# Layer 1 of a two-layer graph attention kernel: the probabilities of 3 of 12 chunks are split in row layout and turned by DMA

## Chip, cores and metric

One core of one Trainium2 chip. The metric is device time in microseconds of the whole launch, lower is better.

## The reference, cut to what matters

```python
x = _layernorm(x + L0(x, L0_gnn_input, adj, L0_gnn_weight))     # x: 6144 x 128, adj: 6144 x 6144
x = _layernorm(x + L1(x, adj, L1_gnn_W, L1_gnn_a1, L1_gnn_a2))

def L0(xx_anchor, input, adj, weight):
    anchor_adj = jnp.einsum('md,de,ne->mn', xx_anchor, weight, input)
    scores = jnp.where(adj > 0, anchor_adj, -2 ** 32 + 1)
    return jax.nn.softmax(scores / 0.07, axis=1) @ input
```

The change lies in L0, which is called layer 1 here (the first of two). Each of its 6144 rows has a softmax over 6144 masked scores and a product of these probabilities with `input`.

## The kernel before

**Layer 1** goes over 48 row tiles of 128 rows. A tile has 6144 scores per row, cut into 12 chunks of 512 (`C = 12`, `CHUNK = 512`, `BPC = 4` blocks of 128 per chunk). Every engine runs its own program (`tile_steps`, on GpSimd `tile_rstd`, on SP `load_tile`) with a body for each tile t and steps c = 0 to 11 in it; semaphores alone couple them, and an engine that waits holds up all that stands behind. One body holds work of three tiles.

- TensorE, `tile_steps` (L484): in step c it turns one chunk of probabilities of an earlier tile (4 transposes through the identity, L502, two PSUM banks `NPT`), makes the scores of chunk c of tile t (L513 to L515, three float16 products, four banks), then the value products of an earlier chunk (`attend`, L467: four times L478 and L480). A chunk of tile t-1 is turned three steps after it would be its turn (`LAG`, `turn_of` L252), and its products follow two steps later (`PV_LAG`). The turn waits for `pT_lo_set` of the chunk two before, which frees its bank. In step 5 it turns the next tile's x (L443).
- ScalarE (L642): copies the turned chunk to float16 (`pT_hi`, L659), then the exponential of chunk c of tile t-1, in place in `rows` (L665, with a sum). In step 5 it copies the finished product out of PSUM (`att`, L653).
- VectorE (L786): on odd c it adds the mask to a pair of score chunks, writes them to `rows` and keeps their maximum (L801). Then `pT_lo` = turned chunk minus `pT_hi` (L810). Then, spread over the steps, masks from the adjacency (L778, steps 0, 2, 4, 10), the sum of probabilities and its inverse (L828, L830, step 3), that inverse over 64 (L833, step 5), residual sums into `xr` (L839, L843, steps 6 and 7), statistics (L847 to L852, step 8), `x1` (L855, step 9), row maximum and exponential's bias (L860, L864, step 11).
- GpSimd, `tile_rstd` (L379): turns each quarter of the mask into bytes (`make_edges`, L360), the power -0.5 for the layer norm (L388), and products for layer 2's scores with a running total (`score_cols`, L371, L377).
- SP: loads x and adj, stores the edge bytes, all in one queue and in the order written (`load_tile`, L294).

**Layer 2** (from about 1070 us) reads the edge bytes back with 48 transposing DMAs (`edgesT`, L322), VectorE makes weights (L891), ScalarE and GpSimd split them (L694, L404), TensorE multiplies. The change doesn't touch it.

Of the kernel before, what the change touches and what calls it, by code (L numbers as in the profile page):

```python
# [10 lines left out]
PT_SLOTS = 4  # L11
PV_LAG = 2
PARTS = 8
PART_SLOTS = 4
# [21 lines left out]
def build(nc, x, adj, inp, w0, w1, a1, a2, edge_rows, out):  # L36
# [17 lines left out]
    with ExitStack() as ctx:  # L54
# [5 lines left out]
        def sem(name):  # L60
            return ctx.enter_context(nc.semaphore(name))
# [28 lines left out]
        pT_hi = sb0("pT_hi", [P, PT_SLOTS, CHUNK], F16)  # L90
        pT_lo = sb0("pT_lo", [P, PT_SLOTS, CHUNK], F16)
        xq = sb0("xq", [P, P], F32)
        xr = sb0("xr", [P, 2, P], F32)
# [115 lines left out]

        x_turned, xT_hi_set, xT_lo_set = sem("x_turned"), sem("xT_hi_set"), sem("xT_lo_set")  # L210
        att_out = sem("att_out")
        max_set, bias_set = sem("max_set"), sem("bias_set")
# [36 lines left out]
        def z_bank(c):  # L249
            return ps[:, (PV, MISC)[c % 2], :]  # L250

        def turn_of(t, c):  # L252

            return (1, c - LAG) if c >= LAG else (2, C - LAG + c)

        def tiles(eng, body):

            for t in range(NB + 2):
                body(t, t % 2, t)
# [4 lines left out]
        def turn_at(known, c):  # L264
            if known is None:
                return True
            off, _ = turn_of(known, c)
            return 0 <= known - off < NB

        def ends_tile(known):  # L270
            return known is None or known >= 2

# [3 lines left out]
        def _(sp):  # L276
# [13 lines left out]
            def store_edges(t, q):  # L290
                sp.wait_ge(edges_set, QUARTERS * t + q + 1)
                sp.dma_start(pair_rows(edge_rows, t)[:, q * QW // 2:(q + 1) * QW // 2], edges[:, q, :]).then_inc(edges_out[q], 16)

            def load_tile(t, par, known):  # L294
                if scores_of(known) and known != 0:

                    after(sp, x_turned, t)
                    sp.dma_start(xq[:], pair_rows(x, t)).then_inc(xq_in, 16)
                    for q in range(QUARTERS):

                        after(sp, mask_set, QUARTERS * (t - 1) + q + 1)
                        sp.dma_start(adj_sb[:, q, :], pair_rows(adj, t)[:, q * QW:(q + 1) * QW]).then_inc(adj_in[q], 16)
                        store_edges(t - 1, q)
                if known == NB:
                    for q in range(QUARTERS):
                        store_edges(t - 1, q)
                if known is None or 1 <= known <= NB:

                    after(sp, x1_set, t - 2)
                    sp.dma_start(xr[:, 1 - par, :], pair_rows(x, t - 1)).then_inc(xr_in[1 - par], 16)  # L310

# [27 lines left out]
        def _(pool):  # L339
# [26 lines left out]
            def score_cols(j):  # L366
# [8 lines left out]
                else:  # L375
                    pool.wait_ge(total_set, j)
                    nc.gpsimd.tensor_tensor(x1_total[:], x1_total[:], x1, ALU.add).then_inc(total_set, 1)  # L377

            def tile_rstd(t, par, known):  # L379
                ahead = t < NB - 1  # L380
                if t < NB:
                    for q in range(QUARTERS // 2, QUARTERS):
                        make_edges(t, q)
                if ahead:
                    make_edges(t + 1, 0)
                if ends_tile(known):
                    pool.wait_ge(ve_set, t - 1)
                    nc.gpsimd.tensor_tensor(small[:, 4:5], small[:, 3:4], consts[:, 0:1], ALU.pow).then_inc(rstd_set, 1)  # L388
                    score_cols(t - 2)
                if ahead:  # L390
                    make_edges(t + 1, 1)
# [36 lines left out]
        def _(pe):  # L428
# [38 lines left out]
            def attend(t_of, bc):  # L467

                n = C * t_of + bc
                pe.wait_ge(pT_lo_set, n + 1)  # L470
                if bc == 0:
                    after(pe, att_out, t_of)
                acc = ps[:, PV, 0:2 * P]
                s = bc % PT_SLOTS
                for b in range(BPC):
                    jb = bc * BPC + b
                    cols = slice(b * P, (b + 1) * P)
                    nc.tensor.matmul(acc, pT_hi[:, s, cols], vals[:, jb, :], start=(jb == 0), stop=False,  # L478
                                     skip_group_check=True)
                    mm = nc.tensor.matmul(acc[:, P:2 * P], pT_lo[:, s, cols], vals[:, jb, 0:P], start=False,  # L480
                                          stop=(jb == NB - 1), skip_group_check=True)
                mm.then_inc(pv_done, 1)

            def tile_steps(t, par, known):  # L484
                for c in range(C):
# [8 lines left out]
                    if turn_at(known, c):  # L494

                        off, bc = turn_of(t, c)
                        pb = par if off == 2 else 1 - par
                        n = C * (t - off) + bc
                        pe.wait_ge(exp_set, C * (t - off) + bc + 1)
                        after(pe, pT_lo_set, n + 1 - NPT)  # L500
                        for b in range(BPC):
                            mm = nc.tensor.transpose(ps[:, PT0 + bc % NPT, b * P:(b + 1) * P],  # L502
                                                     rows[:, pb * N + bc * CHUNK + b * P:pb * N + bc * CHUNK + (b + 1) * P],
                                                     ident[:])
# [12 lines left out]

                    if c < PV_LAG:
                        if known is None or known >= 1 and turn_at(known - 1, C + c - PV_LAG):
                            off, bc = turn_of(t, C + c - PV_LAG)  # L520
                            attend(t - off - 1, bc)
                    elif turn_at(known, c - PV_LAG):
                        off, bc = turn_of(t, c - PV_LAG)
                        attend(t - off, bc)
                    if c == x_step(known) and (known is None or known < NB - 1):
# [86 lines left out]
        def _(act):  # L612
# [29 lines left out]
            def tile_steps(t, par, known):  # L642
                for c in range(C):
                    if known == 0:
                        if c + Z_LEAD + 1 < C:
                            inpT_out(c + Z_LEAD + 1)
                        if c + Z_LEAD < C:
                            z_high(c + Z_LEAD)
                    if c == LAG + PV_LAG and ends_tile(known):

# [3 lines left out]
                    if turn_at(known, c):  # L654
                        off, bc = turn_of(t, c)
                        n = C * (t - off) + bc
                        act.wait_ge(turned, n + 1)
                        after(act, pv_done, n + 1 - PT_SLOTS)
                        nc.scalar.copy(pT_hi[:, bc % PT_SLOTS, :], ps[:, PT0 + bc % NPT, :]).then_inc(pT_hi_set, 1)  # L659
                    if known is None or 1 <= known <= NB:  # L660
# [7 lines left out]
                    if c == x_step(known) and (known is None or known < NB - 1):  # L668
                        xT_high(t + 1, 1 - par)
                    if c == 11 and ends_tile(known):  # L670
                        score_sums(t - 2)

# [75 lines left out]
        def _(dve):  # L748
# [37 lines left out]
            def tile_steps(t, par, known):  # L786
                for c in range(C):
# [5 lines left out]
                    if scores_of(known) and c % 2 == 1:  # L793

                        k = c // 2
                        dve.wait_ge(mask_set, QUARTERS * t + c // QC + 1)
                        after(dve, turned, C * (t - 2) + c + 1 if t >= 2 else 0)
                        if k == 0:
# [5 lines left out]
                    if turn_at(known, c):  # L804

                        off, bc = turn_of(t, c)
                        n = C * (t - off) + bc
                        dve.wait_ge(pT_hi_set, n + 1)
                        s = bc % PT_SLOTS
                        nc.vector.tensor_tensor(pT_lo[:, s, :], ps[:, PT0 + bc % NPT, :], pT_hi[:, s, :],  # L810
                                                ALU.subtract).then_inc(pT_lo_set, 1)
# [13 lines left out]
                    if ends_tile(known):  # L825
# [5 lines left out]
                        if c == 5:  # L831
                            dve.wait_ge(inv_set, t - 1)
                            nc.vector.tensor_scalar(small[:, 2:3], small[:, 1:2], 1.0 / SPLIT_SCALE, None,  # L833
                                                    ALU.mult).then_inc(scaled_set, 1)
                        if c == 6:
                            dve.wait_ge(scaled_set, t - 1)
# [3 lines left out]
                                                           in1=xr[:, par, :], op0=ALU.mult, op1=ALU.add).then_inc(u1_set, 1)  # L840
                        if c == 7:
                            dve.wait_ge(u1_set, t - 1)
                            nc.vector.scalar_tensor_tensor(out=xr[:, par, :], in0=att[:, P:2 * P], scalar=small[:, 2:3],  # L843
                                                           in1=xr[:, par, :], op0=ALU.mult, op1=ALU.add).then_inc(u_set, 1)
                        if c == 8:
                            dve.wait_ge(u_set, t - 1)
                            nc.vector.bn_stats(stats[:], xr[:, par, :]).then_inc(stats_set, 1)  # L847
                            dve.wait_ge(stats_set, t - 1)
                            nc.vector.bn_aggr(moments[:], stats[:]).then_inc(moments_set, 1)
                        if c == 8:  # L850
                            dve.wait_ge(moments_set, t - 1)
                            nc.vector.tensor_scalar(small[:, 3:4], moments[:, 1:2], EPS, None, ALU.add).then_inc(ve_set, 1)  # L852
                        if c == 9:
                            dve.wait_ge(rstd_set, t - 1)
                            nc.vector.tensor_scalar(x1_all[:, t - 2, :], xr[:, par, :], moments[:, 0:1], small[:, 4:5], ALU.subtract,  # L855
                                                    ALU.mult).then_inc(x1_set, 1)
                    if c == C - 1 and scores_of(known):
# [148 lines left out]
```

## Time and profile before

| | |
|---|---|
| median of 3 runs | 1553.66 us (1552.51 to 1554.07) |
| profiled execution | 1552.38 us, its span 1550.5 us |
| TensorE, VectorE, ScalarE, GpSimd busy | 97%, 89%, 70%, 56% of the span |
| DMA | 241 MB, mean 156 GB/s |
| layer 1, layer 2 | up to about 1070 us, about 480 us |

In the profile PE is TensorE, DVE VectorE, ACT ScalarE, POOL GpSimd and SPq the DMA queue of SP. Busy time is the time in which an engine executes; a matmul's end is modelled, and since matmuls are pipelined, the distance between two starts tells more than a duration. The same holds for VectorE, where an instruction's start overlaps the end of the one before by some 0.08 us.

### The profile page before, as it was taken

To read this page: it belongs to the slowest core of one execution; us is meant where nothing else is said; L and a number is where in the kernel's file an instruction comes from. 1 tells how busy PE (TensorE), PEld (TensorE's weight loads), DVE (VectorE), ACT (ScalarE), POOL (GpSimd) and SP (SyncE) were. 2 spreads that over 40 slices of the span, in tenths; PEclk is the share of its full clock that TensorE was granted. 3 is DMA by queue.
4 is the path that set the end of the run, shared out by engine and by line. 5 is a ranking of instruction groups with operands and counts; after the bars stand their busy time and mean duration, and the time that the engine had idled before them with its cause. 6 is when DMAs were issued, how large, how long until landed. Compare 5 with 4: busy or idle time off the path is not lost.

```text
span 1550.5 us, 29603 instructions
## 1 busy us (share of the span) xinstructions
PE 1499.2 (97%) x10429; PEld 1091.5 (70%) x10429; DVE 1383.3 (89%) x2447; ACT 1078.5 (70%) x2423; POOL 864.1 (56%) x580
## 2 busy tenths in 40 slices
PE   6799999999999999999999999997999999999996
PEld 3577777777777777777777777775556666666664
DVE  7999999999999999999999999986869797979794
ACT  3577777777777777777777777777745554546463
POOL 5333344333344333344333343323999999999995
PEclk9999999999999999999999999998999999999998
DMA  7655566555566555565555565524333535353520
GB/s 244 217 166 179 204 211 210 184 173 179 205 211 207 181 175 183 206 211 204 182 173 185 207 211 200 178 74 98 82 65 79 115 62 116 72 109 82 105 61 14
DMA packets 228226, 241.13 MB, mean 156 GB/s; under 512 B 157168, under 2 KB 203504, under 8 KB 228080
## 3 DMA queue, kind: packets, MB, share of 16 engines
q1 hardware_dynamic: 228080, 239.25, 49.9%
q8 instruction: 84, 1.38, 0.4%
q14 instruction: 62, 0.51, 0.1%
HBM read 160.56 MB, written 40.89 MB: 130 GB/s over the span
## 4 chain that ended last, share of the span: by engine, by line
PE 90%; POOL 3%; issue 2%; DVE 1%; ACT 1%; ACTq 0%; POOLq 0%; DVEq 0%
PE ps L502 16%; PE ps L478 16%; PE ps L566 11%; PE ps L559 10%; PE ps L480 8%; PE ps L515 8%; PE ps L514 8%; PE ps L513 8%; PE ps L543 5%; POOL p_lo L404 2%; PE ps L577 1%; POOL vals_lo L400 1%; PE ps L443 0%; PE ps L536 0%; POOL s_prod L371 0%
## 5 line engine op out<-in xcount | busy, mean ns | idle before, releaser
L659 ACT CAST pT_hi<-ps 128x512 f16<-128x512 f32 x576 | 335.0, 582 | 177.0 <-PE ps L502 173.7
L360 POOL TENSOR_SCALAR edges<-neg_mask 128x1536 uint8<-128x1536 bf16 x192 | 283.9, 1479 | 294.6 <-DVE neg_mask L778 290.6
L665 ACT ACTIVATE rows<-rows,exp_bias 128x512 f32<-128x512 f32 x576 | 417.5, 725 | 38.7 <-DVE exp_bias L864 38.7
L478 PE MATMUL ps<-vals,pT_hi 128*128 128x256 f16 x2304 | 442.0, 273 | 0.9 <-ACT att L653 0.8
L404 POOL TENSOR_TENSOR p_lo<-p,p_hi 128x1024 fp32r<-128x1024 f32 x180 | 425.3, 2395 | 13.3 <-PE ps L543 7.7
L480 PE MATMUL ps<-vals,pT_lo 128*128 128x128 f16 x2304 | 411.2, 219 | 0.0
L891 DVE SCALAR_TENSOR_TENSOR p<-ps,e_col,edgesT 128x1024 f32<-128x1024 f32 x288 | 349.0, 1276 | 62.2 <-PE ps L536 37.5
L801 DVE CUSTOM_DVE_ANT_0 rows<-ps,neg_mask 128x1024 f32<-128x1024 f32 x288 | 351.7, 1221 | 52.6 <-PE ps L515 51.4
L810 DVE TENSOR_TENSOR pT_lo<-ps,pT_hi 128x512 f16<-128x512 f32 x576 | 388.8, 682 | 6.5 <-ACT pT_hi L659 6.4
L502 PE MATMUL ps<-ident,rows 128*128 128x128 f32 x2304 | 350.5, 275 | 3.4 <-DVE pT_lo L810 3.2
L694 ACT CAST p_hi<-p 128x1024 fp32r<-128x1024 f32 x180 | 185.2, 1048 | 176.4 <-DVE p L891 174.2
L478 PEld LDWEIGHTS ps<-vals,pT_hi 128*128 128x128 f16 x2304 | 225.4, 98 | 86.8 <-DVE pT_lo L810 1.3
L480 PEld LDWEIGHTS ps<-vals,pT_lo 128*128 128x128 f16 x2304 | 225.5, 98 | 66.1
L502 PEld LDWEIGHTS ps<-ident,rows 128*128 128x128 f32 x2304 | 245.2, 141 | 14.3 <-issue 4.0
L513 PE MATMUL ps<-zT,xT_hi 128*128 128x512 f16 x576 | 219.1, 380 | 5.2 <-DVE vals L764 4.2
L514 PE MATMUL ps<-zT,xT_hi 128*128 128x512 f16 x576 | 219.0, 380 | 0.0
L515 PE MATMUL ps<-zT,xT_lo 128*128 128x512 f16 x576 | 218.8, 380 | 0.0
L566 PE MATMUL ps<-p,vals 128*128 128x512 f32 x432 | 203.4, 593 | 0.0
L778 DVE TENSOR_SCALAR neg_mask<-adj_sb 128x1536 bf16<-128x1536 int32 x192 | 194.2, 1012 | 0.1
L388 POOL TENSOR_TENSOR small<-small,consts 128x1 f32<-128x1 f32 x48 | 26.4, 551 | 269.4 <-DVE small L852 269.4
L559 PE MATMUL ps<-p_hi,vals_hi 128*128 128x512 f32 x360 | 157.3, 518 | 7.5 <-POOL vals_lo L400 4.9
L566 PEld LDWEIGHTS ps<-p,vals 128*128 128x128 f32 x432 | 81.4, 189 | 60.5 <-issue 52.2
(102 smaller groups left out, 1340.3 us busy)
## 6 DMA issues: line engine op xcount, KB each, us to landing
adj_sb<-adj SPq DMA_DIRECT2D x192, 768.0 KB, 6.1
edge_rows<-edges SPq DMA_DIRECT2D x192, 192.0 KB, 5.1
rows<-inp SPq DMA_DIRECT2D x4, 768.0 KB, 9.0
xq<-x SPq DMA_DIRECT2D x48, 64.0 KB, 2.0
xr<-x SPq DMA_DIRECT2D x48, 64.0 KB, 1.8
out<-y_w SPq DMA_DIRECT2D x5, 512.0 KB, 3.6
edgesT<-edge_rows SPq DMA_TRANSPOSE x48, 5.4
out<-y_w SPq DMA_DIRECT2D x2, 256.0 KB, 2.1
```

The source lines that it names most:

```text
L404: nc.gpsimd.tensor_tensor(p1_lo[:, m % LO_SLOTS, :], p1[:, (NB * g + n) % P_SLOTS, :], p1_hi[:, m % HI_SLOTS, :].bitcast(F32), ALU.subtrac ...
L478: nc.tensor.matmul(acc, pT_hi[:, s, cols], vals[:, jb, :], start=(jb == 0), stop=False, skip_group_check=True)
L480: mm = nc.tensor.matmul(acc[:, P:2 * P], pT_lo[:, s, cols], vals[:, jb, 0:P], start=False, stop=(jb == NB - 1), skip_group_check=True)
L502: mm = nc.tensor.transpose(ps[:, PT0 + bc % NPT, b * P:(b + 1) * P], rows[:, pb * N + bc * CHUNK + b * P:pb * N + bc * CHUNK + (b + 1) * P ...
L513: nc.tensor.matmul(scores_bank(c), xT_hi[:, par, :], zT[:, 0, cols], start=True, stop=False)
L514: nc.tensor.matmul(scores_bank(c), xT_hi[:, par, :], zT[:, 1, cols], start=False, stop=False)
L515: nc.tensor.matmul(scores_bank(c), xT_lo[:, par, :], zT[:, 0, cols], start=False, stop=True).then_inc(scored, 1)
L566: mm = nc.tensor.matmul(acc_half(g % 2, i), vals1[:, n, :], p1[:, (NB * g + n) % P_SLOTS, i * CHUNK:(i + 1) * CHUNK], start=(n == 0), stop ...
L665: nc.scalar.activation(row_chunk(1 - par, c), row_chunk(1 - par, c), ACT.Exp, bias=exp_bias[:, 1 - par:2 - par], scale=EXP_SCALE, accum_ou ...
L801: nc.vector.tensor_tensor_reduce(row_pair(par, k), scores_pair(k), neg_mask_row[:, 2 * k * CHUNK:2 * (k + 1) * CHUNK], 1.0, -3.0e38, ALU.a ...
L810: nc.vector.tensor_tensor(pT_lo[:, s, :], ps[:, PT0 + bc % NPT, :], pT_hi[:, s, :], ALU.subtract).then_inc(pT_lo_set, 1)
L891: nc.vector.scalar_tensor_tensor(out=p1[:, (NB * g + n) % P_SLOTS, :], in0=ps[:, R_ROW:R_ROW + 2, :].rearrange("p b w -> p (b w)"), scalar ...
```

## The change

The first three chunks (`MOVED = 3`) of every tile no longer go through TensorE's turn, the copy L659 and the subtraction L810. ScalarE copies the 1536 probabilities to float16 (`moved_hi`), GpSimd subtracts them from `rows` (`moved_lo`), and two transposing DMAs from SBUF to SBUF bring both to `movedT` (two buffers). The other nine chunks are turned in the steps where they were (6 to 11 and 0 to 2), so steps 3 to 5 have no turn. The value products now run through chunks 3 to 11 and then 0 to 2. All that needs the finished product comes three steps later, `x1`, `score_cols` and `score_sums` in the body after, and the loop has one body more. GpSimd's order within a body is edges 2, `score_cols`, edges 3, `moved_low`, edges 0 of the next tile, power, edges 1.

```diff
+MOVED = 3
...
+        TURNS = C - MOVED
+        ATT_STEP = LAG + PV_LAG + MOVED
...
+        def attend_of(t, c):
+            off, i = (1, c - ATT_STEP) if c >= ATT_STEP else (2, C - ATT_STEP + c)
+            return t - off, (i + MOVED) % C
...
         def turn_at(known, c):
...
-            off, _ = turn_of(known, c)
-            return 0 <= known - off < NB
+            off, bc = turn_of(known, c)
+            return 0 <= known - off < NB and bc >= MOVED
...
@@ SP, load_tile: last in the body @@
-                if known is None or 1 <= known <= NB:
-
-                    after(sp, x1_set, t - 2)
-                    sp.dma_start(xr[:, 1 - par, :], pair_rows(x, t - 1)).then_inc(xr_in[1 - par], 16)
+                if 2 <= t <= NB + 1:
+                    tile = t - 2
+                    sp.wait_ge(moved_hi_set, tile + 1)
+                    after(sp, pv_done, C * (tile - 1))
+                    sp.dma_start_transpose(movedT[:, par, 0], moved_hi[:]).then_inc(movedT_in[par], 16)
+                    sp.wait_ge(moved_lo_set, tile + 1)
+                    sp.dma_start_transpose(movedT[:, par, 1], moved_lo[:]).then_inc(movedT_in[par], 16)
...
@@ SP: the load of xr, after the second quarter of adj @@
+                        if q == 1 and t >= 2:
+                            load_xr(t - 2)
...
@@ GpSimd @@
+            def moved_low(tile):
+                pool.wait_ge(moved_hi_set, tile + 1)
+                if tile >= 1:
+                    pool.wait_ge(movedT_in[(tile - 1) % 2], movedT_loads(tile - 1))
+                nc.gpsimd.tensor_tensor(moved_lo[:], rows[:, tile % 2 * N:tile % 2 * N + MOVED * CHUNK], moved_hi[:],
+                                        ALU.subtract).then_inc(moved_lo_set, 1)
...
@@ TensorE, attend @@
+                by_dma = bc < MOVED
+                s = turn_number(t_of, bc) % PT_SLOTS
+                if by_dma:
+                    pe.wait_ge(movedT_in[t_of % 2], movedT_loads(t_of))
+                else:
+                    pe.wait_ge(pT_lo_set, turn_number(t_of, bc) + 1)
...
@@ ScalarE @@
-                    if c == LAG + PV_LAG and ends_tile(known):
+                    if c == ATT_STEP and ends_tile(known):
...
+                    if c == MOVED and 1 <= t <= NB:
+                        act.wait_ge(exp_set, C * (t - 1) + MOVED)
+                        if t >= 2:
+                            act.wait_ge(movedT_in[t % 2], movedT_loads(t - 2))
+                        nc.scalar.copy(moved_hi[:], rows[:, (1 - par) * N:(1 - par) * N + MOVED * CHUNK]).then_inc(moved_hi_set, 1)
...
-                    if c == 11 and ends_tile(known):
-                        score_sums(t - 2)
+                    if c == 4 and t >= 3:
+                        score_sums(t - 3)
...
@@ VectorE: L839 and L843, then L847 to L852, then L855 @@
-                        if c == 6:
+                        if c == ATT_STEP + 1:
...
-                        if c == 7:
+                        if c == ATT_STEP + 1:
...
-                        if c == 8:
+                        if c == ATT_STEP + 2:
...
-                        if c == 9:
-                            dve.wait_ge(rstd_set, t - 1)
...
+                    if c == 0 and t >= 3:
+                        dve.wait_ge(rstd_set, t - 2)
```

## Rows read from the trace of the kernel before

**Rows 1.** Windows: length, busy us of each engine (instructions), TensorE clock, DMA share, GB/s.

```profile
508.53:529.70 21.17, 21.17 (x183) 16.19 (x182) 19.99 (x41) 16.67 (x43) 8.30 (x7) 1.00 0.57 194
```

**Rows 2.** Timeline, TensorE, steps 5 and 6: start us, us, engine, line, operation.

```profile
501.24 0.61 PE L502 MATMUL ps<-ident,rows 128*128 128x128 f32 x4
501.69 0.38 PE L513 MATMUL ps<-zT,xT_hi 128*128 128x512 f16 x1
...
502.33 0.27 PE L478 MATMUL ps<-vals,pT_hi 128*128 128x256 f16 x1
...
503.00 0.28 PE L443 MATMUL ps<-ident,xq 128*128 128x128 f32 x1
503.11 0.60 PE L502 MATMUL ps<-ident,rows 128*128 128x128 f32 x4
```

**Rows 3.** Timeline, VectorE, from step 9 to step 1.

```profile
509.79 1.23 DVE L801 CUSTOM_DVE_ANT_0 rows<-ps,neg_mask 128x1024 f32<-128x1024 f32 x1 [0.20 <-PE ps L515]
...
510.94 0.68 DVE L810 TENSOR_TENSOR pT_lo<-ps,pT_hi 128x512 f16<-128x512 f32 x1
511.54 0.34 DVE L855 TENSOR_SCALAR x_all<-xr,moments,small 128x128 f32<-128x128 f32 x1
...
512.39 1.11 DVE L778 TENSOR_SCALAR neg_mask<-adj_sb 128x1536 bf16<-128x1536 int32 x1
...
514.57 0.68 DVE L810 TENSOR_TENSOR pT_lo<-ps,pT_hi 128x512 f16<-128x512 f32 x1
...
515.35 0.15 DVE L864 TENSOR_SCALAR exp_bias<-row_max 128x1 f32<-128x1 f32 x1
...
516.01 0.95 DVE L778 TENSOR_SCALAR neg_mask<-adj_sb 128x1536 bf16<-128x1536 int32 x1
516.88 1.22 DVE L801 CUSTOM_DVE_ANT_0 rows<-ps,neg_mask 128x1024 f32<-128x1024 f32 x1
```

**Rows 4.** Timeline, TensorE, the turn of step 1.

```profile
515.39 0.63 PE L502 MATMUL ps<-ident,rows 128*128 128x128 f32 x4
```

**Rows 5.** Timeline, VectorE, statistics of step 8, L833 and the second sum.

```profile
508.90 0.28 DVE L847 BATCH_NORM_STATS2 stats<-xr 128x6 f32<-128x128 f32 x1
...
509.43 0.15 DVE L852 TENSOR_SCALAR small<-moments 128x1 f32<-128x1 f32 x1
...
525.80 0.14 DVE L833 TENSOR_SCALAR small<-small 128x1 f32<-128x1 f32 x1
...
529.22 0.34 DVE L843 SCALAR_TENSOR_TENSOR xr<-att,small,xr 128x128 f32<-128x128 f32 x1
529.47 0.68 DVE L810 TENSOR_TENSOR pT_lo<-ps,pT_hi 128x512 f16<-128x512 f32 x1
```

**Rows 6.** Timeline, where GpSimd and VectorE overlap.

```profile
12.38 4.08 POOL L352 TENSOR_SCALAR vals<-rows 128x1536 f16<-128x1536 f32 x1 [0.67 <-DMA rows<-inp]
13.52 3.76 DVE L778 TENSOR_SCALAR neg_mask<-adj_sb 128x1536 bf16<-128x1536 int32 x1
...
512.64 1.18 POOL L377 TENSOR_TENSOR x_total<-x_total,x_all 128x128 f32<-128x128 f32 x1
```

**Rows 7.** The page's groups: line, engine, operation, count, busy us, mean ns, idle before.

```profile
L659 ACT CAST pT_hi<-ps 128x512 f16<-128x512 f32 x576 | 335.0, 582 | 177.0 <-PE ps L502 173.7
...
L404 POOL TENSOR_TENSOR p_lo<-p,p_hi 128x1024 fp32r<-128x1024 f32 x180 | 425.3, 2395 | 13.3 <-PE ps L543 7.7
...
L694 ACT CAST p_hi<-p 128x1024 fp32r<-128x1024 f32 x180 | 185.2, 1048 | 176.4 <-DVE p L891 174.2
```

**Rows 8.** DMA: window as rows 1; issue (min/median/max ns); issues with us to landing.

```profile
1200.00:1400.00 200.00, 200.00 (x740) 133.44 (x739) 169.61 (x208) 103.94 (x133) 193.28 (x89) 1.00 0.43 95
...
L322 SPq DMA_TRANSPOSE edgesT<-edge_rows x48: 2880/3204/4242, 1044.2 to 1487.8; - x48
...
edgesT<-edge_rows SPq DMA_TRANSPOSE x22, 5.4
...
adj_sb<-adj SPq DMA_DIRECT2D x192, 768.0 KB, 6.1
```

More of the change, by code:

```diff
@@ L91, in build @@
         pT_lo = sb0("pT_lo", [P, PT_SLOTS, CHUNK], F16)
+        moved_hi = sb0("moved_hi", [P, MOVED * CHUNK], F16)
+        moved_lo = sb0("moved_lo", [P, MOVED * CHUNK], F16)
+        movedT = sb0("movedT", [P, 2, 2, MOVED * BPC, P], F16)
         xq = sb0("xq", [P, P], F32)
@@ L210, in build @@
         x_turned, xT_hi_set, xT_lo_set = sem("x_turned"), sem("xT_hi_set"), sem("xT_lo_set")
+        moved_hi_set, moved_lo_set = sem("moved_hi_set"), sem("moved_lo_set")
+        movedT_in = [sem(f"movedT_in{i}") for i in range(2)]
         att_out = sem("att_out")
@@ L250, in z_bank, with turn_number, attend_number, movedT_loads @@
             return ps[:, (PV, MISC)[c % 2], :]
+        TURNS = C - MOVED
+        ATT_STEP = LAG + PV_LAG + MOVED
         def turn_of(t, c):
             return (1, c - LAG) if c >= LAG else (2, C - LAG + c)
+        def turn_number(tile, bc):
+            return TURNS * tile + bc - MOVED
+        def attend_number(tile, bc):
+            return C * tile + (bc - MOVED) % C
+        def attend_of(t, c):
+            off, i = (1, c - ATT_STEP) if c >= ATT_STEP else (2, C - ATT_STEP + c)
+            return t - off, (i + MOVED) % C
+        def movedT_loads(tile):
+            return 32 * (tile // 2 + 1)
         def tiles(eng, body):
-            for t in range(NB + 2):
+            for t in range(NB + 3):
                 body(t, t % 2, t)
@@ L266, in turn_at @@
                 return True
-            off, _ = turn_of(known, c)
-            return 0 <= known - off < NB
+            off, bc = turn_of(known, c)
+            return 0 <= known - off < NB and bc >= MOVED
         def ends_tile(known):
-            return known is None or known >= 2
+            return 2 <= known < NB + 2
         block = ctx.enter_context(nc.Block())
@@ L292, in store_edges, with load_xr @@
                 sp.dma_start(pair_rows(edge_rows, t)[:, q * QW // 2:(q + 1) * QW // 2], edges[:, q, :]).then_inc(edges_out[q], 16)
+            def load_xr(tile):
+                after(sp, x1_set, tile - 1)
+                sp.dma_start(xr[:, tile % 2, :], pair_rows(x, tile)).then_inc(xr_in[tile % 2], 16)
             def load_tile(t, par, known):
@@ L303, in load_tile @@
                         store_edges(t - 1, q)
-                if known == NB:
+                        if q == 1 and t >= 2:
+                            load_xr(t - 2)
+                if t == NB:
                     for q in range(QUARTERS):
                         store_edges(t - 1, q)
-                if known is None or 1 <= known <= NB:
-                    after(sp, x1_set, t - 2)
-                    sp.dma_start(xr[:, 1 - par, :], pair_rows(x, t - 1)).then_inc(xr_in[1 - par], 16)
+                    load_xr(t - 2)
+                if 2 <= t <= NB + 1:
[5 more added lines that the diff above has]
+                    sp.dma_start_transpose(movedT[:, par, 1], moved_lo[:]).then_inc(movedT_in[par], 16)
+                if t == NB + 1:
+                    load_xr(t - 2)
             tiles(sp, load_tile)
@@ L381, in tile_rstd @@
                 if t < NB:
-                    for q in range(QUARTERS // 2, QUARTERS):
-                        make_edges(t, q)
+                    make_edges(t, 2)
+                if t >= 3:
+                    score_cols(t - 3)
+                if t < NB:
+                    make_edges(t, 3)
+                if 1 <= t <= NB:
+                    moved_low(t - 1)
                 if ahead:
@@ L388, in tile_rstd @@
                     nc.gpsimd.tensor_tensor(small[:, 4:5], small[:, 3:4], consts[:, 0:1], ALU.pow).then_inc(rstd_set, 1)
-                    score_cols(t - 2)
                 if ahead:
@@ L467, in attend @@
             def attend(t_of, bc):
-                n = C * t_of + bc
-                pe.wait_ge(pT_lo_set, n + 1)
-                if bc == 0:
+                by_dma = bc < MOVED
[4 more added lines that the diff above has]
+                    pe.wait_ge(pT_lo_set, turn_number(t_of, bc) + 1)
+                if bc == MOVED:
                     after(pe, att_out, t_of)
                 acc = ps[:, PV, 0:2 * P]
-                s = bc % PT_SLOTS
                 for b in range(BPC):
@@ L477, in attend @@
                     cols = slice(b * P, (b + 1) * P)
-                    nc.tensor.matmul(acc, pT_hi[:, s, cols], vals[:, jb, :], start=(jb == 0), stop=False,
+                    p_hi = movedT[:, t_of % 2, 0, jb, :] if by_dma else pT_hi[:, s, cols]
+                    p_lo = movedT[:, t_of % 2, 1, jb, :] if by_dma else pT_lo[:, s, cols]
+                    nc.tensor.matmul(acc, p_hi, vals[:, jb, :], start=(bc == MOVED and b == 0), stop=False,
                                      skip_group_check=True)
-                    mm = nc.tensor.matmul(acc[:, P:2 * P], pT_lo[:, s, cols], vals[:, jb, 0:P], start=False,
-                                          stop=(jb == NB - 1), skip_group_check=True)
+                    mm = nc.tensor.matmul(acc[:, P:2 * P], p_lo, vals[:, jb, 0:P], start=False,
+                                          stop=(bc == MOVED - 1 and b == BPC - 1), skip_group_check=True)
                 mm.then_inc(pv_done, 1)
@@ L497, in tile_steps @@
                         pb = par if off == 2 else 1 - par
-                        n = C * (t - off) + bc
+                        n = turn_number(t - off, bc)
                         pe.wait_ge(exp_set, C * (t - off) + bc + 1)
@@ L501, in tile_steps @@
                         for b in range(BPC):
-                            mm = nc.tensor.transpose(ps[:, PT0 + bc % NPT, b * P:(b + 1) * P],
+                            mm = nc.tensor.transpose(ps[:, PT0 + n % NPT, b * P:(b + 1) * P],
                                                      rows[:, pb * N + bc * CHUNK + b * P:pb * N + bc * CHUNK + (b + 1) * P],
@@ L516, in tile_steps @@
                                          stop=True).then_inc(scored, 1)
[L518 to L524, printed above, removed]
+                    tile, bc = attend_of(t, c)
+                    if 0 <= tile < NB:
+                        attend(tile, bc)
                     if c == x_step(known) and (known is None or known < NB - 1):
@@ L655, in tile_steps @@
                         off, bc = turn_of(t, c)
-                        n = C * (t - off) + bc
+                        n = turn_number(t - off, bc)
                         act.wait_ge(turned, n + 1)
-                        after(act, pv_done, n + 1 - PT_SLOTS)
-                        nc.scalar.copy(pT_hi[:, bc % PT_SLOTS, :], ps[:, PT0 + bc % NPT, :]).then_inc(pT_hi_set, 1)
+                        if n >= PT_SLOTS:
+                            act.wait_ge(pv_done, attend_number((n - PT_SLOTS) // TURNS, (n - PT_SLOTS) % TURNS + MOVED) + 1)
+                        nc.scalar.copy(pT_hi[:, n % PT_SLOTS, :], ps[:, PT0 + n % NPT, :]).then_inc(pT_hi_set, 1)
+                    if c == MOVED and 1 <= t <= NB:
[3 more added lines that the diff above has]
+                        nc.scalar.copy(moved_hi[:], rows[:, (1 - par) * N:(1 - par) * N + MOVED * CHUNK]).then_inc(moved_hi_set, 1)
                     if known is None or 1 <= known <= NB:
@@ L796, in tile_steps @@
                         dve.wait_ge(mask_set, QUARTERS * t + c // QC + 1)
-                        after(dve, turned, C * (t - 2) + c + 1 if t >= 2 else 0)
+                        if t >= 2:
+                            if 2 * k < MOVED:
+                                dve.wait_ge(moved_lo_set, t - 1)
+                            if c >= MOVED:
+                                dve.wait_ge(turned, turn_number(t - 2, c) + 1)
                         if k == 0:
@@ L806, in tile_steps @@
                         off, bc = turn_of(t, c)
-                        n = C * (t - off) + bc
+                        n = turn_number(t - off, bc)
                         dve.wait_ge(pT_hi_set, n + 1)
-                        s = bc % PT_SLOTS
-                        nc.vector.tensor_tensor(pT_lo[:, s, :], ps[:, PT0 + bc % NPT, :], pT_hi[:, s, :],
+                        s = n % PT_SLOTS
+                        nc.vector.tensor_tensor(pT_lo[:, s, :], ps[:, PT0 + n % NPT, :], pT_hi[:, s, :],
                                                 ALU.subtract).then_inc(pT_lo_set, 1)
@@ L849, in tile_steps @@
                             nc.vector.bn_aggr(moments[:], stats[:]).then_inc(moments_set, 1)
-                        if c == 8:
+                        if c == ATT_STEP + 2:
                             dve.wait_ge(moments_set, t - 1)
                             nc.vector.tensor_scalar(small[:, 3:4], moments[:, 1:2], EPS, None, ALU.add).then_inc(ve_set, 1)
-                        if c == 9:
-                            dve.wait_ge(rstd_set, t - 1)
-                            nc.vector.tensor_scalar(x1_all[:, t - 2, :], xr[:, par, :], moments[:, 0:1], small[:, 4:5], ALU.subtract,
-                                                    ALU.mult).then_inc(x1_set, 1)
+                    if c == 0 and t >= 3:
+                        dve.wait_ge(rstd_set, t - 2)
+                        nc.vector.tensor_scalar(x1_all[:, t - 3, :], xr[:, 1 - par, :], moments[:, 0:1], small[:, 4:5],
+                                                ALU.subtract, ALU.mult).then_inc(x1_set, 1)
                     if c == C - 1 and scores_of(known):
```

## The prediction

> **What bounds the kernel now.** I read the page first, then its windows, then the timeline of one tile. The attention loop over 48 row tiles runs to about 1070 us. In the length of one tile, 21.17 us, TensorE is busy throughout, VectorE for 20.0 us, ScalarE for 16.7, GpSimd for 8.3, the DMA engines for 0.57 of the time [rows 1]. So TensorE sets the tile: see in the timeline that a step is 0.44 us of turning, 0.65 of scores, 0.66 of value products, 1.75 in all, and 0.11 for the turn of x in step 5 [rows 2]. 12 x 1.75 + 0.11 = 21.11. The missing 0.06 is the second thing to see: TensorE's turn of step 1 starts at 515.39, not at 515.36 as the rhythm would have it, because VectorE's low part of step 11 starts at 514.57 and its turn bank is free 0.82 us later [rows 3, 4]. VectorE has 1.2 us of slack per tile but none at this place. That decides what the change is worth.
>
> **What is removed.** Three chunks of twelve are no longer turned by TensorE: 3 x 0.44 = 1.32 us per tile [rows 2]. Steps 3, 4 and 5 lose their turn (1.31 us each), and VectorE and ScalarE lose three instructions each (VectorE 3 x 0.60 by start to start, ScalarE 3 x 0.48 or more [rows 3, 7]). Alone that is a tile of 21.11 - 1.32 = 19.79 us.
>
> **What is moved.** The value products of chunks 0 to 2 come last, so att is complete three steps later, and the two sums into xr go from steps 6 and 7 to step 9, the statistics from 8 to 10, x1 from 9 to 0. I walk VectorE through the new order with start-to-start times: L801 1.15, L810 0.60, a free L778 0.87 [rows 3], the first sum 0.37 (0.34 and its own result awaited) and the second 0.25, the statistics 0.60 in all [rows 5]. Zero is TensorE's start of step 9. L801 of step 9 begins at 1.43, as now; L810 at 2.58; the sums at 3.18 and 3.55; L810 of step 10 at 3.80; mask 4.40; statistics 5.27; L801 of step 11 at 5.87; L810 at 7.02. The turn of step 1 cannot start before 7.02 + 0.83 = 7.85, and its nominal time is 7.00. So 0.85 us of the 1.32 is given back by a stall of TensorE in step 1. After it the steps follow each other: 3.50 for steps 1 and 2, 4.04 for 3 to 5, 5.25 for 6 to 8, which puts the next step 9 at 20.64. VectorE on the way: L810 of step 0 at 7.87, mask 8.47, x1 9.34, L801 of step 1 at 9.59, L810s 10.74 and 11.34, mask 11.94 (held up to 12.2 by GpSimd's x1_total), L801 of step 3 at about 13.1, the sum of probabilities and its inverse 0.27, mask of the next tile ready at 14.5. GpSimd's edges of the mask before run to 14.8 by then, so the mask runs 14.8 to 15.7; L801 of step 5 15.7 to 16.8; xT_low; then the tiny L833 (x/64 of the inverse) at 17.0.
>
> **What is added.** ScalarE gets one copy of 128x1536. Between L659 (512 elements, 582 ns) and L694 (1024, 1048 ns) one element costs 0.91 ns, so about 1.5 us [rows 7]. With the moved score sums (about 0.65) it has 5.1 us to do in steps 3 to 5, of 4.0; it enters them 0.3 late and is in time again by step 7, and the copy for step 6 ends as VectorE gets there. Nothing on the path, and 16.7 us busy leave room.
> GpSimd gets one subtraction of 128x1536 (moved_low). No row shows it. Nearest are L404, two float32 inputs, 2395 ns for 1024, which makes 3.59 us, and L352, one input but float16 out, 4.08 us for 1536 [rows 6, 7]. I take 3.85 and keep both ends. It runs behind edges 3 and behind the mask that waited for them, from 15.7 to 19.3 (19.8), and delays edges 0 of the next tile to about 21.3. GpSimd has the time, and what waits for it is only its store. The rstd comes after step 10 and finds it idle.
> DMA gets two transposes of 393 KB. One edgesT transpose (1024x384, 2 bytes) moves as much as both. 22 of them in 200 us of the second layer take a share of 0.43: 86 / 22 = 3.9 us of all 16 engines [rows 8]. 0.57 x 21.18 + 3.9 = 16.0 us of some 21: room. On SP the waits for moved_hi and moved_lo stand ahead of the loads of xq and of the first quarter of adj for the tile after next. SP is through at about 20 + 1.6 (half of the 3.2 us issue of edgesT); the mask that needs the quarter comes near 36. Landing takes 6.1 us, and 5.4 for what is ahead [rows 8]. Hidden, with some 3 us over. movedT is read a tile after it is issued, so TensorE's new wait costs nothing. The last tile's products end three steps (2 us) later, the first body has them fewer; I count 0, ends -2 and +2. The rest of the kernel (second layer, 480 us) is not touched.
>
> **Where GpSimd and VectorE meet.** Rows 6 show what a long GpSimd instruction does: the mask L778 started at 13.52, took 3.76 us instead of 0.95 and ended 0.8 after GpSimd's L352 did. The other way too: x_total took 1.18 us beside the mask of 512.39, which itself took 0.16 more than a free one. L810 and L801 are never held. moved_low is a new GpSimd instruction of 3.6 to 4.1 us, and inside it falls VectorE's L833. It is the same kind of instruction as the mask (tensor_scalar, from SBUF to SBUF, immediate operands), but with one element per partition, and in this trace no such tiny one meets GpSimd's work by more than 0.02 us (L864 at 515.35 [rows 3, 6]). By the nearest row, L778, it is held to the end of moved_low.
> The Trainium skill ("SBUF — State Buffer", section "SBUF: two separate sides") says the same of the long ones: a VectorE instruction in a two-port mode and a GpSimd instruction exclude each other for the whole instruction. Its rule for who is in such a mode ("Vector Engine (DVE) Microarchitecture Reference", section 5.1) asks for SBUF on both sides and an even or equal count, which does not leave out a count of one; no row here shows it.
> If L833 is held, it goes at 19.3 to 19.8, L810 of step 6 follows at 19.38 to 19.87, and the turn of step 8, nominal 18.89, waits for it until 20.21 to 20.70. The next step 9 is at 21.96 to 22.45, middle 22.2. Against 21.18 the tile is 0.78 to 1.27 longer, middle 1.02. VectorE's idle 1 us after it is lost because the burst of steps 9 to 1 cannot be begun early.
>
> **The sum.** 46 bodies are in full rhythm (2 to 47): 46 x 1.02 = +47 us. The profiled execution is 1552.38 us (span 1550.5), 1.3 under the median 1553.66. 1553.7 + 47 = 1600.7; I say 1600, with 1590 to 1612 as this case's own range.
>
> **Rivals.** (1) The tiny instruction is not held (faster). Then the tile is 20.64, 0.54 less: 46 x 0.54 = 25, so 1529; with the step-1 stall between 0.5 and 1.0, 1514 to 1536. For it: one element may need no second port. Against: the same kind of instruction waits in rows 6. It decides at nothing but this. (2) The mask at 14.5 loses its race with moved_low: it must be waiting when edges 3 ends (14.8). Then it is held to 18.4, L801 and L810 follow at 19.3 and 20.7, the turn of step 8 waits to 21.5 (2.6 late), tile 23.3: +97, 1650. It decides when VectorE comes 0.3 us later; unlikely, as VectorE lags here and does not wait for scores. (3) The transposes from SBUF cost three times as much (11.7 us): 23.8 us of DMA per tile, 1675. At twice the price still nothing. (4) No stall in step 1 and none at L833: 46 x 1.39 = 64, 1490; rows 3 and 4 speak against. (5) A part of the gain of (1) is eaten by small holds: 1536 to 1565.
>
> **How the numbers follow.** Forecast 0.43, (1) 0.40, (2) 0.07, (3) 0.03, (4) 0.02, (5) 0.05. The range 1514 to 1616 takes in the forecast and (1) with their bounds and (5). A measurement of this kernel tells about 0.2% from no change. Faster by more: 0.40 + 0.02 + 0.01 = 0.43; within: 0.04; slower: 0.43 + 0.07 + 0.03 = 0.53.
>
> **What would show it.** L833: 0.14 us now; 2.4 or more in the forecast, 0.14 in rival 1. TensorE's idle per tile: before the turn of step 1 0.85 us for "DVE pT_lo", before that of step 8 1.3 to 1.8 in the forecast only. The distance of two L833s is the tile: 22.2, 20.6, or 23.3 with a mask of over 4 us. GpSimd's moved_low 3.6 to 4.1; if it is 6, all of the held cases grow by 2 us per tile. Waits for adj_sb or for movedT would speak for rival 3. Wrong altogether would be this reading if the sums in step 9 did not push L810 of step 11 past 7 us after the start of step 9.

## The result, and the profile after

| | before | after |
|---|---|---|
| median | 1553.81 us (1552.51 to 1554.07) | 1532.55 us (1532.11 to 1532.88) |
| ratio | | 0.9866, 95% interval 0.9851 to 0.9881 |
| span of the profiled execution | 1550.5 us | 1530.3 us |
| TensorE, VectorE, GpSimd busy | 97%, 89%, 56% | 94%, 85%, 66% |

Faster by 21 us, where 47 us slower was forecast. Rival 1 (1529 us) is what happened. The window of one tile in the changed kernel (columns as in [rows 1]):

```profile
497.78:518.55 20.77, 19.97 (x172) 14.90 (x171) 18.49 (x37) 16.39 (x41) 11.30 (x8) 1.00 0.95 260
```

The distance from one tile to the next fell from 21.18 to 20.77 us (median over the L833s and the L889s), and TensorE, busy throughout in [rows 1], now stands still for 0.80 us of it. 46 tiles x 0.41 are 18.9 us of the 20.2 by which the span shrank. Start and end of the loop make the rest: the first L833 (now L889) comes 4.6 us earlier, at 76.2 instead of 80.82, and what is left, some 3.3 us, goes back at the end. That this is the last tile's products, which finish three steps later, was not measured apart.

Where TensorE stands: the turn of step 1, and VectorE's way to it. Timelines of VectorE and TensorE of the changed kernel from step 9 (L857 was L801, L866 was L810, L830 was L778, L895 and L899 were L839 and L843):

```profile
497.78 1.23 DVE L857 CUSTOM_DVE_ANT_0 rows<-ps,neg_mask 128x1024 f32<-128x1024 f32 x1 [1.07 <-PE ps L565]
...
499.54 0.34 DVE L895 SCALAR_TENSOR_TENSOR xr<-att,small,xr 128x128 f32<-128x128 f32 x1
499.91 0.35 DVE L899 SCALAR_TENSOR_TENSOR xr<-att,small,xr 128x128 f32<-128x128 f32 x1
500.18 0.68 DVE L866 TENSOR_TENSOR pT_lo<-ps,pT_hi 128x512 f16<-128x512 f32 x1
500.78 0.95 DVE L830 TENSOR_SCALAR neg_mask<-adj_sb 128x1536 bf16<-128x1536 int32 x1
501.64 0.29 DVE L903 BATCH_NORM_STATS2 stats<-xr 128x6 f32<-128x128 f32 x1
...
502.33 1.23 DVE L857 CUSTOM_DVE_ANT_0 rows<-ps,neg_mask 128x1024 f32<-128x1024 f32 x1
...
503.48 0.69 DVE L866 TENSOR_TENSOR pT_lo<-ps,pT_hi 128x512 f16<-128x512 f32 x1
```

```profile
504.32 0.63 PE L552 MATMUL ps<-ident,rows 128*128 128x128 f32 x4 [0.80 <-DVE pT_lo L866]
```

VectorE waits 1.07 us for the scores of step 9, and from then on it runs without a gap until the low part of step 11 at 503.48; TensorE has waited 0.80 us for it. This run of work without a gap is called the burst below. In [rows 3] only x1 stood there beside the mask, and in [rows 4] the turn was 0.03 late.

These were to meet in step 5: GpSimd's moved_lo and VectorE's tiny L889 (timelines of GpSimd and of VectorE):

```profile
509.73 1.47 POOL L394 TENSOR_SCALAR edges<-neg_mask 128x1536 uint8<-128x1536 bf16 x1 [0.98 <-DVE neg_mask L830]
511.28 3.70 POOL L417 TENSOR_TENSOR moved_lo<-rows,moved_hi 128x1536 f16<-128x1536 f32 x1
```

```profile
510.93 1.08 DVE L830 TENSOR_SCALAR neg_mask<-adj_sb 128x1536 bf16<-128x1536 int32 x1
...
513.27 0.14 DVE L889 TENSOR_SCALAR small<-small 128x1 f32<-128x1 f32 x1
```

L889 runs at 513.27 in the middle of moved_lo (511.28 to 514.98) and takes its 0.14 us as in [rows 5]; so do all 46 L889s that fall inside a GpSimd instruction, of 48. The mask ahead of moved_lo is of 1536 elements, and it was held and did hold, as in [rows 6]: it takes 1.08 us instead of 0.95, since it waited for the edges' end, and moved_lo's 3.70 us begin with the rest of the mask. The shortest moved_lo of the run took 3.11 us.

### The profile page after: what moved, and what is told of

Read it like the earlier page. It is cut to its first block, busy times and chain, and to the rows that moved or that the text cites. A ratio compares the mean times of both kernels' runs of the same rounds, so it can differ in the third digit from the quotient of the medians.

```text
span 1530.3 us, 28253 instructions
## 1 busy us (share of the span) xinstructions
PE 1442.6 (94%) x9853; PEld 1030.4 (67%) x9853; DVE 1308.3 (85%) x2303; ACT 1065.1 (70%) x2327; POOL 1009.0 (66%) x628
## 4 chain that ended last, share of the span: by engine, by line
PE 70%; DVE 16%; issue 6%; POOL 3%; ACT 1%; DVEq 0%; ACTq 0%; POOLq 0%
PE ps L612 11%; PE ps L528 11%; PE ps L605 10%; PE ps L552 9%; PE ps L565 6%; PE ps L564 6%; PE ps L563 6%; DVE pT_lo L866 6%; PE ps L530 5%; PE ps L589 5%; DVE rows L857 4%; DVE neg_mask L830 3%; POOL p_lo L449 2%; DVE xr L895 1%; PE ps L623 1%
## 5 line engine op out<-in xcount | busy, mean ns | idle before, releaser
L857 DVE CUSTOM_DVE_ANT_0 rows<-ps,neg_mask 128x1024 f32<-128x1024 f32 x288 | 350.7, 1218 | 99.7 <-PE ps L565 99.1
L706 ACT CAST pT_hi<-ps 128x512 f16<-128x512 f32 x432 | 252.0, 583 | 129.6 <-PE ps L552 121.6
L528 PE MATMUL ps<-vals,pT_hi 128*128 128x256 f16 x1728 | 331.4, 273 | 1.2 <-ACT att L699 0.8
L530 PE MATMUL ps<-vals,pT_lo 128*128 128x128 f16 x1728 | 308.3, 219 | 0.0
L552 PE MATMUL ps<-ident,rows 128*128 128x128 f32 x1728 | 263.0, 275 | 39.7 <-DVE pT_lo L866 39.0
L866 DVE TENSOR_TENSOR pT_lo<-ps,pT_hi 128x512 f16<-128x512 f32 x432 | 287.1, 682 | 8.7 <-ACT pT_hi L706 8.7
L552 PEld LDWEIGHTS ps<-ident,rows 128*128 128x128 f32 x1728 | 184.4, 141 | 54.0 <-issue 45.8
L528 PEld LDWEIGHTS ps<-vals,pT_hi 128*128 128x128 f16 x1728 | 169.1, 98 | 65.9 <-DVE pT_lo L866 1.9
L530 PEld LDWEIGHTS ps<-vals,pT_lo 128*128 128x128 f16 x1728 | 169.1, 98 | 49.4
L830 DVE TENSOR_SCALAR neg_mask<-adj_sb 128x1536 bf16<-128x1536 int32 x192 | 201.3, 1048 | 0.5 <-POOL edges L394 0.3
L417 POOL TENSOR_TENSOR moved_lo<-rows,moved_hi 128x1536 f16<-128x1536 f32 x48 | 176.4, 3675 | 6.5 <-ACT moved_hi L711 2.7
```

The lines of the kernel that those rows point to most:

```text
L528: nc.tensor.matmul(acc, p_hi, vals[:, jb, :], start=(bc == MOVED and b == 0), stop=False, skip_group_check=True)
L530: mm = nc.tensor.matmul(acc[:, P:2 * P], p_lo, vals[:, jb, 0:P], start=False, stop=(bc == MOVED - 1 and b == BPC - 1), skip_group_check=True)
L552: mm = nc.tensor.transpose(ps[:, PT0 + n % NPT, b * P:(b + 1) * P], rows[:, pb * N + bc * CHUNK + b * P:pb * N + bc * CHUNK + (b + 1) * P] ...
L857: nc.vector.tensor_tensor_reduce(row_pair(par, k), scores_pair(k), neg_mask_row[:, 2 * k * CHUNK:2 * (k + 1) * CHUNK], 1.0, -3.0e38, ALU.a ...
L866: nc.vector.tensor_tensor(pT_lo[:, s, :], ps[:, PT0 + n % NPT, :], pT_hi[:, s, :], ALU.subtract).then_inc(pT_lo_set, 1)
```

## The experiments

Eight kernels are the changed kernel with an edit, e5 is the kernel before with one. Where an edit adds a line, the lines behind it stand one further down (L858 is L857, L867 is L866, L418 is L417, L890 is L889). Ratios are to the kernel before. Theory: VectorE's burst between steps 9 and 11 is what TensorE waits for in step 1, and an instruction of one element per partition is not held by GpSimd. Rivals: the DMA engines, VectorE's total, or another reason for the mask's holds.

**e1: the second mask in step 8**, where VectorE stands idle for 1.07 us.

```diff
-                        if c in (4, 10) and (known is None or known < NB - 1):
-                            make_mask(t + 1, c // 10, None)
+                        if c in (4, 8) and (known is None or known < NB - 1):
+                            make_mask(t + 1, c // 8, None)
```

> The changed kernel with one move: VectorE makes the next tile's second mask in step 8 instead of step 10, where it stands idle for 1.07 us. Theory (the burst of steps 9 to 11 on VectorE gives back 0.80 us per tile as a stall of TensorE in step 1): the mask's 0.87 us leaves the burst, the low part of step 11 starts 6.3 us after step 9 instead of 7.1, the stall shrinks from 0.80 to about 0.1 us, the tile from 20.77 to 19.9 us, the whole to about 1493 us. Rival (the DMA engines, busy for 0.87 to 0.95 of the time now, are the next bound and take the gain): waits for adj_sb or movedT appear, the tile stays above 20.4 us, the whole above 1515.

1493.98 us (1493.24 to 1494.48), ratio 0.9613 (0.9598 to 0.9627). Window of 600 us, first the changed kernel, then e1:

```profile
300.00:900.00 600.00, 576.59 (x4878) 429.96 (x4877) 533.06 (x1069) 472.93 (x1155) 325.68 (x231) 1.00 0.88 235
```

```profile
300.00:900.00 600.00, 599.72 (x5097) 448.96 (x5095) 556.33 (x1114) 493.51 (x1205) 338.40 (x240) 1.00 0.90 245
```

This is what the theory said. TensorE's idle of 23.4 us has gone, at a DMA share of 0.90 instead of 0.88, and the tile is 19.90 us. One instruction in another place was worth 39 us, more than the change itself.

**e3 and e4: two bn_stats more** on VectorE, at the end of step 10 or of step 6.

```diff
+                    if c == 10 and ends_tile(known):        # e4: c == 6
+                        for i in range(2):
+                            nc.vector.bn_stats(probe[:, i, 0:6], ident[:])
```

> The changed kernel plus two bn_stats of 128 elements on VectorE at the end of step 10, inside the burst, some 0.41 us together; their output is not used. Theory (the burst is what TensorE waits for in step 1): the stall grows one for one from 0.80 to 1.2 us, 47 x 0.41 = 19 us, 1552 us. Rival (the stall has another cause, such as the turn's copy on ScalarE): within 3 us of 1532.5.

> The same two bn_stats at the end of step 6, where VectorE then stands idle for about 1 us before the scores of step 7. Theory (what counts is the place, not VectorE's busy time): no change, 1532.5 within 2 us. Rival (VectorE's total is the bound): as much longer as with the same work in step 10, 1552 us.

e3: 1546.73 us (1546.16 to 1547.70), e4: 1533.27 us (1533.17 to 1533.33), the changed kernel 1532.55. In the burst the two cost 14.2 us, elsewhere 0.7. That is 14.2 / 47 = 0.30 us per tile. VectorE's burst in e3, and TensorE's turn of step 1:

```profile
508.41 0.15 DVE L909 TENSOR_SCALAR small<-moments 128x1 f32<-128x1 f32 x1
508.48 0.48 DVE L912 BATCH_NORM_STATS2 probe<-ident 128x6 f32<-128x128 f32 x2
508.88 1.21 DVE L858 CUSTOM_DVE_ANT_0 rows<-ps,neg_mask 128x1024 f32<-128x1024 f32 x1
```

```profile
510.84 0.63 PE L553 MATMUL ps<-ident,rows 128*128 128x128 f32 x4 [1.09 <-DVE pT_lo L867]
```

From L909 to L858 it is 0.47 us, against 0.14 without them (502.19 to 502.33): 0.33 us more. TensorE's wait grows from 0.80 to 1.09 us, and 0.30 us per tile arrive in the time. e3 was expected at 1552 us because the two were taken as 0.41 us; the mechanism held, nearly one for one.

**e2: instructions of L889's kind in rising width** behind it.

```diff
+                            for i, width in enumerate((1, 2, 3, 8, 32, 128)):
+                                nc.vector.tensor_scalar(probe[:, i, 0:width], ident[:, 0:width], 0.5, None, ALU.mult)
```

> The changed kernel plus six extra VectorE instructions of L889's kind (tensor_scalar, SBUF to SBUF, float32, immediate) right behind it in step 5, where GpSimd's moved_lo runs: 1, 2, 3, 8, 32 and 128 elements per partition in this order; their output is not used. Theory (only a count of one escapes the hold): the first and none of the others takes its free time; the one of 2 ends with moved_lo, some 1.6 us later, the rest then run free, TensorE stalls about 0.6 us more per tile, 1555 to 1570 us. Rival (float32 instructions of this kind are never held, whatever their width, and the masks are held for another reason): all six take under 0.2 us, 1533 us. Second rival (a short instruction slips through, a long one not): the held one is that of 32 or 128.

1623.40 us, ratio 1.0446. Groups by shape, columns as in [rows 7]:

```profile
L893 DVE TENSOR_SCALAR probe<-ident 128x2 f32<-128x2 f32 x48 | 74.2, 1546 | 0.0
L893 DVE TENSOR_SCALAR probe<-ident 128x128 f32<-128x128 f32 x48 | 67.9, 1414 | 0.0
L893 DVE TENSOR_SCALAR probe<-ident 128x32 f32<-128x32 f32 x48 | 8.1, 168 | 0.0
...
L893 DVE TENSOR_SCALAR probe<-ident 128x1 f32<-128x1 f32 x48 | 6.6, 138 | 0.0
```

The one of 1 element took 138 ns. The one of 2 took 1546 ns in the mean: 46 of 48 met moved_lo, and each of them was held to its end (1.58 us or more), the other two met nothing and took 0.16. Those of 3, 8 and 32 started in the 0.1 us between moved_lo and the edges behind it, so they say nothing about width; that of 128 was then held by the edges. So 1 is not held, 2, 128 and the mask's 1536 are; whether it is the count of one or an odd count that goes free, no run shows. The second hold was not foreseen, and the total lies 53 us above the upper end of what was expected.

**e7: one of 2 elements alone**, the case that was forecast.

> The changed kernel with one more instruction behind L889, the same operation on 2 elements per partition; its output is not used. It stands in for an L889 that is held, the case that was forecast. Theory (the forecast's mechanism, but from where moved_lo really ends, 18.6 us after step 9 and not 19.3 to 19.8): held for 1.6 us, the low part of step 6 follows at 18.6 + 0.1, the turn of step 8 waits until 19.5 instead of 19.0, the tile is 21.25 us, the whole 1555 us. Rival (the forecast's own sum): a tile of 22.0 us or more, 1590 us or more.

1549.67 us (1548.75 to 1550.17), ratio 0.9975 (0.9966 to 0.9985). VectorE and GpSimd:

```profile
521.89 0.14 DVE L890 TENSOR_SCALAR small<-small 128x1 f32<-128x1 f32 x1
521.95 1.67 DVE L892 TENSOR_SCALAR probe<-ident 128x2 f32<-128x2 f32 x1
523.53 0.68 DVE L867 TENSOR_TENSOR pT_lo<-ps,pT_hi 128x512 f16<-128x512 f32 x1
```

```profile
519.90 3.69 POOL L418 TENSOR_TENSOR moved_lo<-rows,moved_hi 128x1536 f16<-128x1536 f32 x1
```

TensorE's turn of step 8:

```profile
524.36 0.63 PE L553 MATMUL ps<-ident,rows 128*128 128x128 f32 x4 [0.18 <-DVE pT_lo L867]
```

The one of 2 elements is held for 1.5 us, to moved_lo's end at 523.59. The run takes 17 us more than the changed kernel, 0.37 per tile. The theory had 1555 us; the rival, the forecast's own sum with 1.3 to 1.8 us of stall, had 1590 or more. In e2 an instruction of 1 element in this same place, right behind L890, was not held, so it is the width and not the place or the output that differs.

**e5: the early mask in the kernel before.**

> The kernel before with the second mask in step 8 instead of 10, the change itself left out. Theory (there VectorE's burst costs only 0.06 us per tile, and all else is TensorE's own work): at most 48 x 0.06 = 3 us, so 1551 to 1554 us. Rival (the early mask is worth its 39 us by itself and has nothing to do with the change): about 1515 us.

1577.77 us (1576.68 to 1578.39), ratio 1.0156 (1.0140 to 1.0173): slower, which neither theory nor rival expected. VectorE in steps 8 and 9, and TensorE's turn of step 11:

```profile
499.34 0.68 DVE L810 TENSOR_TENSOR pT_lo<-ps,pT_hi 128x512 f16<-128x512 f32 x1
499.94 0.95 DVE L778 TENSOR_SCALAR neg_mask<-adj_sb 128x1536 bf16<-128x1536 int32 x1
500.81 0.28 DVE L847 BATCH_NORM_STATS2 stats<-xr 128x6 f32<-128x128 f32 x1
...
502.64 0.69 DVE L810 TENSOR_TENSOR pT_lo<-ps,pT_hi 128x512 f16<-128x512 f32 x1
```

```profile
503.47 0.63 PE L502 MATMUL ps<-ident,rows 128*128 128x128 f32 x4 [0.41 <-DVE pT_lo L810]
```

There the statistics stand in step 8, the mask joins them, the low part of step 9 is late and the turn of step 11 starts 0.83 us behind it after a wait of 0.41 us. The tile is 21.72 us, 0.54 more than before. Step 8 became a free place only through the change, which moved the sums and statistics away from it.

**e6, e8 and e9: four chunks moved**, with the early mask; in e8 GpSimd also makes the second quarter's edges ahead of the power. e9 is e8 with three chunks.

```diff
-MOVED = 3
+MOVED = 4
...
                     make_edges(t + 1, 0)          # e8 and e9, GpSimd
+                    make_edges(t + 1, 1)
...
-                if ahead:
-                    make_edges(t + 1, 1)
```

> The changed kernel with the early mask and four chunks moved instead of three. By TensorE alone the tile would be 19.91 - 0.44 = 19.47 us and the whole 1473 us. The DMA share of the changed kernel, 0.877 of 20.77 us, is 18.2 us per tile against 12.1 before, so a moved chunk costs about 2.0 us of all 16 engines. Theory (the DMA engines are the next bound): 12.1 + 4 x 2.0 = 20.2 us per tile, waits for adj_sb or movedT appear, the whole is 1500 to 1512 us, slower than with three chunks (1494). Rival (they still have room, the share counts waiting too): 1470 to 1480 us.

> Four chunks moved, the early mask, and on GpSimd the edges of the second quarter ahead of the power instead of behind it, so that they no longer run where VectorE makes the third mask. Theory (with four chunks the 1549 us come from a mask of step 0 held 1.3 us and from VectorE's burst, not from the DMA engines): the mask of step 0 takes 0.95 us again, the tile falls from 21.19 to 19.9 us or less, the whole to 1475 to 1495 us. Rival (the DMA engines at 0.89 of the time are at their limit): the tile stays at or above 21 us and waits for adj_sb or movedT appear.

> The same order on GpSimd with three chunks and the early mask. Theory (there TensorE is busy for 599.7 of 600 us, so VectorE's and GpSimd's order no longer matters): 1494 us within 2. Rival (some stall of TensorE is hidden in what the trace shows as busy): 1485 us or less.

e6: 1551.31 us (1551.04 to 1552.46), ratio 0.9990. Both sides missed. The DMA share stayed at 0.89 and TensorE and VectorE never waited for a transfer; the mask of step 0 was held by the edges, and TensorE's value products then waited 1.11 us for VectorE's low part:

```profile
511.95 2.23 DVE L830 TENSOR_SCALAR neg_mask<-adj_sb 128x1536 bf16<-128x1536 int32 x1
```

```profile
516.23 0.28 PE L528 MATMUL ps<-vals,pT_hi 128*128 128x256 f16 x1 [1.11 <-DVE pT_lo L866]
```

e8, with these edges out of the way: 1494.61 us (1494.21 to 1495.04), ratio 0.9625, at the upper end of what was expected. e9, the same with three chunks: 1493.78 us (1493.00 to 1494.71), ratio 0.9621, no different from e1. Window of e8:

```profile
300.00:900.00 600.00, 588.34 (x4966) 432.58 (x4964) 563.20 (x1082) 484.43 (x1174) 368.61 (x242) 1.00 0.98 258
```

In this order a fourth chunk brings nothing more: TensorE stands for 11.7 of 600 us, the DMA engines are busy for 0.98 of the time. Its waits are all for VectorE's low part, one of 0.39 us per tile (502.70), none for a transfer; ahead of it stands the mask of step 8, held by GpSimd's edges:

```profile
498.93 1.89 DVE L829 TENSOR_SCALAR neg_mask<-adj_sb 128x1536 bf16<-128x1536 int32 x1
```

So VectorE's order is again what the trace shows as the limit. What the DMA engines would allow if this mask were free was not run.

## Why the prediction was wrong, point by point

- **What bounds the kernel, and the removed work**: right. TensorE's busy time per tile fell by 1.20 us (21.17 to 19.97; 1.32 of turning less the modelled ends).
- **The stall in step 1**: right in place and cause, a little small. The turn comes 7.97 us after step 9 and not 7.85, mostly because the statistics take 0.69 and not 0.60. Counted as the prediction counts, from the nominal 7.00, the stall is 0.97 us and not 0.85; the profile's 0.80 is shorter because the modelled end of the matmul before it covers 0.17. So the tile is 20.77 and not 20.64, and rival 1 reads 1529 where 1532.55 was measured. e1 and e3 show that it is this stall: without the mask in the burst it is gone, with 0.33 us more it grows by 0.30.
- **Whether L833 is held**: wrong, the first of two steps that failed. "By the nearest row, L778, it is held." It was not: 0.14 us inside moved_lo. The nearest row was of the same operation, but with 1536 elements. e2 and e7 measured what separates them: 1 element 0.14 us, 2 elements held to the end. That of the two readings the dearer was taken at 0.43 against 0.40 was a coin's toss: in the trace of the kernel before, no tensor_scalar of one element from SBUF to SBUF meets a GpSimd instruction by more than 0.10 us (L864 by 0.03 and once by 0.10, where the prediction read 0.02).
- **How much a held instruction costs**: wrong too, and by itself enough for the wrong sign. moved_lo was taken as 3.59 to 4.08 us, from 15.7 after step 9; it is 3.11 without a hold, and it ended at 18.6 (514.98 less 496.35; step 9 starts at 496.35), not at 19.3 to 19.8. With a hold of 1.5 us the tile grows by 0.37 us, not by 1.3 to 1.8 (e7). So as far as e7 stands in for a held L833, the kernel would have been 0.25% faster even then, not 3% slower. An end of the range should have gone below the nearest rows too: the stall is a difference of two large numbers, and 0.7 us of error in one is most of it.
- **ScalarE**: right. Its copy takes 1.47 us (1.5 forecast) and delays nothing.
- **The mask's race with moved_lo** (rival 2): right that the mask wins. It takes 1.08 us.
- **DMA**: the conclusion held, the price did not. 0.57 x 21.17 = 12.1 us per tile became 0.88 x 20.77 = 18.3, so the pair costs 6.2 us of all 16 engines and not 3.9. In the window of 300 to 900 us the trace's packets of 256 bytes, which only the transposes have there, take 0.244 of the engines' time, 5.1 us per tile. The rest is mostly adj's packets of 6144 bytes, which take 322 ns in the mean beside them and 289 before. Landing is fast enough (adj_sb 4.9 us, before 6.1 [rows 8]):

```profile
movedT<-moved_hi SPq DMA_TRANSPOSE x48, 5.5
movedT<-moved_lo SPq DMA_TRANSPOSE x48, 3.8
```

- **Start and end of the loop**: taken as 0, measured 1.3 us of gain, inside the bounds.

## What to carry to other kernels

Walk the engine that is almost full through the new order with start-to-start times: work moved off the bound engine is worth only what the next engine's order lets through, and here one mask two steps earlier was worth nearly twice as much as the change (e1). The same move in the old order cost 24 us (e5), so look for a free place again after each change. Where a forecast hangs on whether one tiny instruction waits, and no row shows one of its size, say that the case is open, and price the wait as a difference with both ends wide before letting it set the sign.

## What the hardware showed that was not expected

A VectorE tensor_scalar from SBUF to SBUF on one element per partition runs beside a GpSimd instruction (138 ns), the same on two elements waits for its end (1605 ns in the median of e2; every one of the 46 that met moved_lo, in e2 and in e7). The Trainium skill's condition for the two-port mode ("Vector Engine (DVE) Microarchitecture Reference", section 5.1) asks for an even count, or an odd one that is the same on both sides. If that is read to take in a count of one, the measurement says otherwise; for two it agrees.
A transposing DMA from SBUF to SBUF takes the DMA engines 5.1 / 0.79 = 6.4 us per MB in its own packets, and 6.2 / 0.79 = 7.9 with what the others lose beside it; the plain loads and stores of this loop took 12.1 / 4.1 = 3.0 before. The Trainium skill ("Advanced Engine Details and Errata", section "X-Bar Transpose (TRN2)") calls transposing DMAs as fast as regular ones; by the engines' busy time in this kernel they are not.
